# Sort steps beside the gather stream in instructions of at most 512 columns, and another pace for the work beside it

## The reference, cut to what matters

```
out_deg = minimum(segment_sum(ones, src), 511); in_deg = minimum(segment_sum(ones, dst), 511)
edge_proj = edge_attr @ W_sum + b_sum            # 200000 edges x 128 attributes
sum3d = segment_sum(edge_proj, src)              # needs the edges grouped by src
x = x + (norm(x) + z_in[in_deg] + z_out[out_deg] + cent_term + vor_term + sum3d)
```

## Time and profile before

| | |
|---|---|
| median of three runs | 6188.05 us |
| profiled execution | 6193.96 us, its span 6192.2 us |
| busy in the span | VectorE 4715.9 us (76%), POOL 3585.2 us (58%), TensorE 2914.5 us (47%), ScalarE 915.0 us (15%) |
| stream: first to last gather | 264.5 us to 2423.3 us |

### The profile page before, as it was taken

One profiled execution on the slowest core, in us unless ns is written; L12 is line 12 of the kernel. 1 busy time (PEld: TensorE's weight loads), 2 busy tenths in 40 slices (PEclk: granted clock), 3 DMA queues, 4 the chain that ended last, 5 costly groups with the idle time before them and its releaser, 6 DMA issues. The chain is left out here.

```text
span 6192.2 us, 42233 instructions
## 1 busy us (share of the span) xinstructions
PE 2914.5 (47%) x12286; PEld 2230.7 (36%) x12286; DVE 4715.9 (76%) x8203; ACT 915.0 (15%) x2337; POOL 3585.2 (58%) x3612
## 2 busy tenths in 40 slices
PE   0001444443001100799999444444444444445798
PEld 0001443443001100566666333333333333334565
DVE  8798767667989942666663699999999999997533
ACT  0000111111101110333232011111111111111222
POOL 0266777777777776422220577777777777775000
PEclk9999999999975555899999777777777777777899
DMA  0243444443222233112110688888888888885000
GB/s 10 73 134 128 159 153 153 153 153 116 89 89 91 89 114 103 39 56 66 54 48 30 193 267 269 267 263 270 269 265 266 269 269 264 267 269 170 28 18 18
DMA packets 341480, 929.06 MB, mean 150 GB/s; under 512 B 85372, under 2 KB 124571, under 8 KB 341120
## 3 DMA queue, kind: packets, MB, share of 16 engines
q0 software_dynamic: 200048, 591.98, 32.6%
q1 hardware_dynamic: 97568, 175.50, 8.0%
q10 hardware_dynamic: 43632, 158.88, 6.6%
HBM read 666.26 MB, written 259.83 MB: 150 GB/s over the span
## 5 line engine op out<-in xcount | busy, mean ns | idle before, releaser
L552 POOL DMA_INDIRECT big<-in_edge_attr,big x1568 | 1635.3, 1043 | 778.7 <-issue 462.3
L1593 POOL DMA_INDIRECT big<-keys_values,idx x1712 | 1622.2, 948 | 521.8 <-issue 511.7
L1751 PE MATMUL bank<-big,ident 128*128 128x264 f32 x3424 | 1027.2, 471 | 1132.1 <-DVE big L1656 1108.3
L1751 PEld LDWEIGHTS bank<-big,ident 128*128 128x128 f32 x3424 | 805.0, 239 | 1354.1 <-DVE big L1656 1152.3
L758 DVE SCALAR_TENSOR_TENSOR bank<-bank,big 128x128 f32<-128x128 f32 x1566 | 560.9, 358 | 446.6 <-DMA big<-in_edge_attr,big 397.4
L781 PE MATMUL bank<-big 128*128 128x64 bf16 x3200 | 406.1, 302 | 539.3 <-DVE big L626 539.3
L781 PEld LDWEIGHTS bank<-big 128*128 128x128 bf16 x3200 | 378.5, 146 | 566.9 <-DVE big L626 563.1
L1684 DVE TENSOR_TENSOR big<-big,bank 128x1024 f32<-128x1024 f32 x428 | 493.6, 1215 | 54.3 <-DMA big<-keys_values,idx 54.0
L816 ACT ACTIVATE big<-bank 128x512 f32<-128x512 f32 x392 | 234.9, 599 | 1953.3 <-DVE bank L758 1944.9
L1708 DVE TENSOR_TENSOR big<-big,bank 128x1056 f32<-128x1056 f32 x428 | 507.8, 1248 | 4.0 <-ACT bank L1770 0.3
L271 PE MATMUL bank<-ident,big 128*128 128x128 f32 x224 | 53.0, 425 | 911.2 <-DVE big L218 911.2
(11 more groups left out here) (346 smaller groups left out, 3897.6 us busy)
## 6 DMA issues: line engine op xcount, KB each, us to landing
running_sums<-big ACTq DMA_DIRECT2D x196, 512.0 KB, 2.8
running_attention<-big SPq DMA_DIRECT2D x107, 544.0 KB, 4.6
queries_by_row<-big ACTq DMA_DIRECT2D x107, 512.0 KB
big<-queries_by_row SPq DMA_DIRECT2D x107, 512.0 KB, 6.0
big<-keys_values,idx POOLq DMA_INDIRECT x1712, 3.9
big<-in_edge_attr,big POOLq DMA_INDIRECT x1568
keys_values<-big SPq DMA_DIRECT2D x7, 1820.0 KB
x_after_layer<-big SPq DMA_DIRECT2D x7, 896.0 KB, 5.7
```

The source lines that it names most:

```text
L552: pool.indirect_dma_start(out=z.rows[:, r, k, :], out_offset=None, in_=w["edge_attr_128"][:, :], in_offset=bass.IndirectOffsetOnAxis(ap=z. ...
L1593: pool.indirect_dma_start(out=kv[:, r, k, :], out_offset=None, in_=t["kv"][:, :], in_offset=bass.IndirectOffsetOnAxis(ap=m.idx2[:, c:c + 1 ...
L1751: mm = pe.matmul(weighted(i), lhsT=m.ident[:, :], rhs=kv[:, b % RINGK, i * S + j, D:KW], start=(j == 0), stop=(j == S - 1), skip_group_che ...
```

## The change

Four edits. In sorts with `copies` each step over a width of 2048 is cut into pieces of max(1024, 2d) columns; each piece is a min and a max over half of them. Only the last instruction of a step raises `s_step`. A sort of width 1024 is cut into one piece, so its instructions are as before. The cost of a step in these sorts is 3.0 in place of 2.5 (for width 2048), of a one-hot pair 1.6 in place of 1.9, and the pace after each batch is 7.8 in place of 8.6.

```diff
-    each = 2.5 * plan.width / KC
+    each = (3.0 if copies else 2.5) * plan.width / KC
...
+    def pieces(src, dst, d):
+
+        wide = plan.width if not copies else max(1024, 2 * d)
+        for lo in range(0, plan.width, wide):
+            yield halves(src[:, lo:lo + wide], d), halves(dst[:, lo:lo + wide], d)
+
     def step(d, mirrored):
-        src, dst = halves(plan.buf(n), d), halves(plan.buf(n + 1), d)
         dve.wait_ge(s_step, plan.base + n)
-        if mirrored:
-            v.tensor_tensor(dst[:, :, 0, :], src[:, :, 0, :], src[:, :, 1, ::-1], ALU.min)
-            v.tensor_tensor(dst[:, :, 1, :], src[:, :, 1, :], src[:, :, 0, ::-1], ALU.max).then_inc(s_step, 1)
-        else:
-            v.tensor_tensor(dst[:, :, 0, :], src[:, :, 0, :], src[:, :, 1, :], ALU.min)
-            v.tensor_tensor(dst[:, :, 1, :], src[:, :, 0, :], src[:, :, 1, :], ALU.max).then_inc(s_step, 1)
+        for src, dst in pieces(plan.buf(n), plan.buf(n + 1), d):
+            low, high = src[:, :, 0, :], src[:, :, 1, :]
+            if mirrored:
+                v.tensor_tensor(dst[:, :, 0, :], low, high[:, :, ::-1], ALU.min)
+                ins = v.tensor_tensor(dst[:, :, 1, :], high, low[:, :, ::-1], ALU.max)
+            else:
+                v.tensor_tensor(dst[:, :, 0, :], low, high, ALU.min)
+                ins = v.tensor_tensor(dst[:, :, 1, :], low, high, ALU.max)
+        ins.then_inc(s_step, 1)
...
-                    yield 1.9
+                    yield 1.6
...
-                spent = spend(8.0 + 8.6 * (b + 1), spent)
+                spent = spend(8.0 + 7.8 * (b + 1), spent)
```

## The result

The changed kernel takes 6052.4 us (median of five runs, 6048.12 to 6054.88) against 6187.34 us of the kernel before (five runs): ratio 0.9776, 95% interval 0.9765 to 0.9786. The profiled execution has a span of 6046.4 us; its last gather starts at 2284.7 us, 138.6 us sooner than before.

The account below looks back on a forecast made before the run. POOL's chain of gathers was taken as the bound: floor 1959.1 us, gathers' waits 100 and buffers 4 gave 2063 against 2159.7; with 2 us at the end, net -95 from 6188, 6093 us. Range 6062 to 6150 us.

Parts of the forecast that it names:

- Waits for stored sums: POOL's waits for a free buffer, mostly in the sort of width 1024: 4 us in place of 46, bounds 0 and 20.
- The pair 10.55 against 10.58 us a batch: Sort of width 1024 after the change: VectorE's time against POOL's for a batch, taken as level.
- Sort of width 1024: Gathers' waiting beside this sort, same instructions more thinly dealt: 264 gathers at 0.072 us, 19 us, bounds 13 and 24.
- One-hots: Gathers' waiting beside the one-hots: the same 400 pairs in 82 batches in place of 88, 34 us as before.
- what a gather loses there: Gathers' waiting in the sort of width 2048: 46 us in place of 100, bounds 17 and 84.
- the count from the seams: Sort of width 2048, lower bound: only the first gather of each batch's side work waits, about 0.03 us a gather, 17 us.
- VectorE's price of the cut: Sort of width 2048: four instructions take 2.55 us, +0.16 us a step, 25 us in all, off the path.
- Where the side work ends: Counted from the yields: side work lasts 192.7 of 196 batches, against 172.8 before.
- shorter instructions don't help the gathers: Rival: the sort of width 2048 still loses 100 us and only the pace pays, -41 us, 6147 us; 9 in 100.
- its second ground: The skill's inferred sentence that `tensor_tensor` doesn't stall GpSimd's DMAs, leaving the 100 us as other waits; 2 in 100.
- VectorE binds in both sorts: Rival: lumps keep the ring full in the first sort and the end sticks out, -65 us, 6123 us; 6 in 100.
- Every seam is missed: Rival, sort of width 2048: gathers in side work each wait 0.56 us, 207 us, +66 us, 6254 us; 4 in 100.

Follow-up runs that it names:

- pace_alone: The changed kernel with uncut steps of 1024 columns, so new costs and pace only: 6142.9 us against 6191.7 for the kernel before, ratio 0.9925.
- cut_with_waits: The changed kernel with VectorE waiting for its own last instruction between the two pieces of each cut step: 6067.8 us, ratio 0.9800.
- cut_alone: The changed kernel with the old costs and pace, only the step instructions cut: 6186.7 us against 6191.7 for the kernel before, ratio 0.9993.
- pace_alone_2: Second run, on another device, of the changed kernel with uncut steps: 6145.1 us against 6196.7 for the kernel before, ratio 0.9917.
- changed_3: The changed kernel itself, run again as the measure for later variants: 6058.0 us, ratio 0.9783 to the kernel before.
- triples_4: The changed kernel with one-hots of two groups made by three 1024-column instructions in place of four: 6032.1 us, ratio 0.9739 to the kernel before.
- onehot_triples: The changed kernel with one-hots of two groups made by three instructions, on a slower device: 6844.9 us against 6795.3 for the kernel before, ratio 1.0068.

## Why the prediction was wrong

*Bound and mechanism: right.* Gathers on POOL bound the stage, a gather waits for the rest of the instruction it starts in, and of the terms above the floor the two that were forecast to move did: the gathers' loss in the sort of width 2048 from 100 to 14 us, the waits for buffers from 46 to nothing.

*Waits for stored sums:* 4 us expected, 0.3 measured; before, 52.6 with the ordinary gaps. Right, 4 us too careful. The pair 10.55 against 10.58 us a batch held without a reserve: pace_alone, too, has no such wait over 0.3 us.

*Sort of width 1024:* 19 us expected, 14 measured. *One-hots:* 34 expected, 31 measured.

*Sort of width 2048: the failed step.* The term "what a gather loses there" was mis-sized: 46 us taken (42 and 4 for the flips), 14 measured. I took the mean of the half-length sort of width 1024 as the nearest row, and had beside it, as the lower bound, the count from the seams: 17 us. The count's number is near, its picture only in part: it let the first gather of a batch wait and every later one meet a seam, where the timeline has every second one lose 0.08 us. The nearest row was near in length and not in spacing: its two instructions take 1.33 us with the wait at a step's end, and a gather comes 0.08 us too early each time. With four instructions a step, two gathers find 2.57 us. cut_with_waits gives the new sort the spacing of the old one and gets its loss back: 0.995 us a gather, 29 us. That term is 32 of the 43 us by which the stream was missed, the other three 5, 3 and 4 (rounded).

*VectorE's price of the cut:* +0.16 us a step expected by start-to-start times (2.55 us), 2.57 us measured. The sum of durations (+0.31 us) would have been wrong. That it is covered held. cut_alone shows what happens where it is not: with the old pace VectorE is the slower of the two throughout the last sort, and the whole gain of the gathers is lost, not only the 25 to 48 us that the forecast named as the price.

*Where the side work ends:* 192.7 batches counted; it ends ahead of batch 193.

*The range:* the lower ends of the terms gave -39 us, 6054 us, and I allowed only -31; the one-hots had no lower end at all. The stream was 43 us faster than forecast, the time 41.

*The signs:* under 15 us of waits for stores and the end ahead of batch 193 came; the mean of 1.02 us in the last sort (0.969) and the last gather near 2328 us (2284.7) did not.

*Rivals:* "shorter instructions don't help the gathers" is refuted by pace_alone against the changed kernel, 87 us apart on one device (pace_alone_2 and changed_3). With it goes its second ground, that the waits are of another origin: they move with the spacing of the step instructions. "VectorE binds in both sorts" did not come (0.3 us of waits for stored sums, nothing left for the end). "Every seam is missed" did not come: the closeness of 1.81 and 1.83 us, which spoke for it, was what kept the gathers in step instead.

## What to carry to other kernels

When a string of equal GpSimd DMAs runs beside two-input VectorE instructions, look at the period of the DMAs (here 1.25 us) and at the distances between VectorE's starts, not only at the length, which bounds what one miss costs (1.04 us in the earlier trace rows): two starts that add up to just short of the period (2 x 0.605 us) cost 0.006 to 0.024 us a gather, the same instructions at 1.33 us for two 0.050, and instructions of half that length 0.074. Shortening what delays one engine pays only where the other has time for it; deal out the side work by measured costs first, then cut. A nearest row for an unknown cost has to be near in what decides the cost.

## What the runs showed of the hardware that was not expected

- The hold goes both ways: a gather in a seam delays VectorE's next two-input instruction by about 0.04 us, and that keeps the two in step (4 us lost by 651 gathers in triples_4).
- The kernel before took about 6190 us on some devices and 6795 to 6842 us on three others. Each device was met in one session only, so device and time of day are not told apart. On the slower ones packets of the GpSimd queue were about as long (mean 164 ns in onehot_triples against 161 in the changed kernel, worked out from the queue's share of the engines' time), but TensorE, ScalarE and VectorE had unexplained gaps ahead of instructions, and a gain of 2.2% measured on one device was none on the other.
